# A ViT tower in fp32 on one core: the patch embedding on 64 rows in paired row halves, its bias added apart

## The reference, cut to what matters

```python
h  = patches @ W.T + b                            # (16, 784, 64): the embedding
xn = layernorm(h)                                 # over the 64 features
s_t = tanh(xn_t @ W_ih.T + b_ih + b_hh + s_(t-1) @ W_hh.T)   # scan over the 16 images
h  = h + s
x  = layernorm(h)
logits = x @ gate_w + gate_b                      # top 2 of 16, softmax over the two
e_out[e] = relu(x @ w1[e] + b1[e]) @ w2[e] + b2[e]
y  = x + sum over the 2 chosen e of weight * e_out[e]
out = h + layernorm(y) * gamma + beta
```

## Time and profile before

| | |
|---|---|
| median of 3 runs | 536.03 us |
| profiled execution, whole time | 535.65 us |
| its span in the trace | 533.9 us |
| mean granted clock of TensorE | 0.989 |
| PE busy | 507.5 us, 95% |
| DVE busy | 418.0 us, 78% |
| ACT busy | 350.3 us, 66% |
| POOL busy | 173.6 us, 33% |

### The profile page before, as it was taken

The page is one execution under the profiler, slowest core; times in us unless marked ns, Lnnn a source line. Parts: engine busy times, 40 slices in busy tenths (PEclk is TensorE's granted clock), DMA queues, the critical chain, the costliest instruction groups (busy, mean ns, idle before and its releaser), DMA issues.

```text
span 533.9 us, 8845 instructions
## 1 busy us (share of the span) xinstructions
PE 507.5 (95%) x3044; PEld 338.5 (63%) x3044; DVE 418.0 (78%) x841; ACT 350.3 (66%) x606; POOL 173.6 (33%) x126
## 2 busy tenths in 40 slices
PE   4777999999999999999999999999999999999992
PEld 4454667676766766666676666667676766666652
DVE  1545797896969788796969889696988879797665
ACT  3545575857768586766858675776858577666661
POOL 4220111613424252432335162332426244222223
PEclk9997999999999999999999999999999999999998
DMA  6219175855829194573909476482928456483901
GB/s 142 67 40 221 40 170 130 189 124 121 175 70 229 40 208 102 125 182 93 211 25 206 104 171 144 103 192 63 219 59 187 109 129 151 110 189 77 205 19 30
DMA packets 29755, 69.04 MB, mean 129 GB/s; under 512 B 6432, under 2 KB 8464, under 8 KB 29584
## 3 DMA queue, kind: packets, MB, share of 16 engines
q1 hardware_dynamic: 29712, 68.49, 56.2%
HBM read 60.39 MB, written 8.08 MB: 128 GB/s over the span
## 4 chain that ended last, share of the span: by engine, by line
PE 89%; issue 3%; POOL 2%; DMA 2%; DVE 1%; ACT 1%; POOLq 0%; SPq 0%; DVEq 0%; ACTq 0%
PE pZ L845 37%; PE pO L858 34%; PE pA L871 4%; PE pA L760 3%; PE pA L796 2%; PE pA L814 2%; PE pB L760 2%; PE pA L784 2%; PE pB L826 1%; POOL inv_std L348 1%; DMA spread<-gates_dram 1%; PE pB L814 1%; PE pA L772 1%; PE pA L785 1%; DMA gates_dram<-gt 1%
## 5 line engine op out<-in xcount | busy, mean ns | idle before, releaser
L478 ACT ACTIVATE hexp<-pZ,b1c 128x784 f32<-128x784 f32 x256 | 223.1, 911 | 107.2 <-PE pZ L845 107.1
L858 PE MATMUL pO<-hexp,w2s 128*64 128x392 f32 x1024 | 199.8, 506 | 0.6 <-ACT hexp L478 0.3
L845 PE MATMUL pZ<-xt,w1hi 128*128 128x392 f32 x512 | 189.2, 369 | 1.4 <-ACT xt L405 1.0
L637 DVE SCALAR_TENSOR_TENSOR prod<-pO,b2c,spread 128x392 f32<-128x392 f32 x256 | 149.0, 620 | 42.3 <-PE pO L858 38.6
L845 PE MATMUL pZ<-xt,w1lo 128*128 128x392 f32 x512 | 175.4, 343 | 0.0
L348 POOL TENSOR_TENSOR inv_std<-var,nhalf 112x7 f32<-112x7 f32 x48 | 75.8, 1580 | 198.0 <-DVE var L546 198.0
L845 PEld LDWEIGHTS pZ<-xt,w1hi 128*128 128x128 f32 x512 | 97.2, 190 | 48.1 <-issue 28.7
L858 PEld LDWEIGHTS pO<-hexp,w2s 128*64 128x64 f32 x1024 | 70.3, 136 | 75.9 <-issue 63.1
L653 DVE TENSOR_TENSOR acc<-acc,prod 128x784 f32<-128x784 f32 x111 | 111.3, 1003 | 0.1
L845 PEld LDWEIGHTS pZ<-xt,w1lo 128*128 128x128 f32 x512 | 97.4, 190 | 0.0
L546 DVE TENSOR_REDUCE var<-sq 112x7 f32<-112x455 f32 x48 | 29.9, 624 | 49.2 <-ACT sq L409 36.4
(11 more groups left out here) (95 smaller groups left out, 472.7 us busy)
## 6 DMA issues: line engine op xcount, KB each, us to landing
spread<-gates_dram SPq DMA_DIRECT2D x128, 392.0 KB, 9.0
h_dram<-h SPq DMA_DIRECT2D x16, 248.1 KB, 2.4
h2c<-h_dram SPq DMA_DIRECT2D x16, 248.1 KB, 7.2
xcur<-x_in SPq DMA_DIRECT2D x16, 196.0 KB, 7.2
out<-yo SPq DMA_DIRECT2D x15, 196.0 KB, 7.0
w1f<-w SPq DMA_DIRECT2D x2, 512.0 KB, 5.9
w2s<-w SPq DMA_DIRECT2D x1, 512.0 KB, 3.7
gates_dram<-gt SPq DMA_DIRECT2D x16, 28.0 KB, 2.0
```

Of the source, the lines that this page charges most:

```text
L478: nc.scalar.activation(hexp[u % RING][:, :].rearrange("p (b c) -> p b c", b=2), halves(pZ[u % 2]), ACT.Relu, bias=b1c[:, u:u + 1]).then_in ...
L637: nc.vector.scalar_tensor_tensor(out=prod[q % RING][:, b * HALF:(b + 1) * HALF], in0=halves(pO)[:, b, :], scalar=b2c[:, q:q + 1], in1=spre ...
L845: last = nc.tensor.matmul(halves(pZ[e % 2])[:, b, :], w[:, e, :], xt[par][:, b * HALF:(b + 1) * HALF], start=(k == 0), stop=(k == 1))
L858: last = nc.tensor.matmul(halves(pO)[k * D:(k + 1) * D, b, :], w2s[:, e, :], hexp[e % RING][:, b * HALF:(b + 1) * HALF], start=True, stop= ...
```

## The change: what it does, and the diff

The embedding is over the 64 pixel rows alone. `xcur` has 128 rows: the even tiles' tokens lie on the rows 0 to 63, the odd tiles' on the rows 64 to 127 (the host lays them out in that order, and `load_x` issues two DMAs, of 448 and 336 columns). `tokw` stands on both row halves, made by two products in place of one. The bias, turned through `fold` like the weights, is made by one more product as a tile `tokb` of 112 x 81 and copied by DVE. In the loop ACT still copies the result to `h1`, and POOL then adds `tokb` to it in place (`bias_h1`, ahead of `rstd` of the mix stage). In the prologue DVE does the copy and the addition in one instruction for each bank, in place of ACT's copy. `square_h1` moves from slot 11 to 13 (from 12 in body 0), and the embedding's `norm_var` from slot 13 to 14. The two fills of the row of ones go.

```diff
-        tokw = sb("tokw", [K_IN + 1, W])
+        tokw = sb("tokw", [2 * D, W])
+        tokb = sb("tokb", [P, W])
...
-        xcur = [sb(f"xcur{i}", [K_IN + 1, TOK]) for i in range(2)]
+        xcur = [sb(f"xcur{i}", [2 * D, FIRST]) for i in range(2)]
...
-        fills = [(fold[:, 0:D], -1.0 / D), (fold[:, D:D + 1], 1.0 / D), (xcur[0][K_IN:K_IN + 1, :], 1.0),
-                 (xcur[1][K_IN:K_IN + 1, :], 1.0),
+        fills = [(fold[:, 0:D], -1.0 / D), (fold[:, D:D + 1], 1.0 / D),
                  (ident[:, :], 0.0), (sq[:, :, :, D:D + 1], EPS), (nhalf[:, :], -0.5), (state[:, :, :], 0.0),
                  (gates[:, :, :], 0.0)]
-        FOLD_SET, ONES_SET, EPS_SET, STATE_SET = 4, 6, 8, 10
+        FOLD_SET, EPS_SET, STATE_SET = 4, 6, 8
         RANK_SET, IDENT_SET = len(fills) + 3, len(fills) + 4
...
-                sp.dma_start(xcur[s % 2][0:K_IN, :], x_in[:, bass.ds(s * TOK, TOK)]).then_inc(xload[s % 2], 16)
+                for k, (first, n) in enumerate(((0, FIRST), (FIRST, REST))):
+                    sp.dma_start(xcur[s % 2][k * D:(k + 1) * D, 0:n],
+                                 x_in[:, bass.ds(s * TOK + first, n)]).then_inc(xload[s % 2], 16)
...
+            def bias_h1(s, par):
+
+                pool.wait_ge(h1_kept, 2 * s + 2)
+                nc.gpsimd.tensor_tensor(h1[par][:, :, :], h1[par][:, :, :], over_tiles(tokb[:, :], W), ALU.add)\
+                    .then_inc(h1_biased, 1)
...
+                if embed:
+                    bias_h1(t + 3, 1 - par)
...
-                for some, fresh in zip(some_tiles, embedded_in(s)):
+                for some, fresh in zip(some_tiles, wide):
...
-                act.wait_ge(h1_kept, 2 * (s) + 2)
+                if known(s, 3):
+                    act.wait_ge(h1_kept, 2 * s + 2)
+                else:
+                    act.wait_ge(h1_biased, s - 2)
...
-                    if embed and u == at(t, 11, first=12):
+                    if embed and u == 13:
...
-            nc.scalar.activation(tokw[:, :], pB[0:K_IN + 1, 0:W], ACT.Copy).then_inc(weights_made, 1)
-            keep_h1(0, 0)
+            nc.scalar.activation(tokw[:, :], pB[:, 0:W], ACT.Copy).then_inc(weights_made, 1)
             square_h1(0, 0)
-            keep_h1(1, 1)
             square_h1(1, 1)
             w1_high_part(0)
...
-            keep_h1(2, 0)
...
+            def keep_h1(s, par):
+
+                dve.wait_ge(h1_made, s + 1)
+                if not known(s, 2):
+                    STATE.wait(dve, s - 2, "h2")
+                for some, n, fresh in zip(some_tiles, (PAIRS, TILES - PAIRS), embedded_in(s)):
+                    nc.vector.tensor_tensor(h1[par][:, some, :], fresh, tokb[:, :].unsqueeze(1).to_broadcast([P, n, W]),
+                                            ALU.add).then_inc(h1_kept, 1)
...
-                    if embed and u == 13:
+                    if embed and u == 14:
...
+            dve.wait_ge(weights_made, 3)
+            nc.vector.tensor_copy(tokb[:, :], pA[0:P, 0:W]).then_inc(tokb_made, 1)
+            dve.wait_ge(tokb_made, 1)
+            keep_h1(0, 0)
             dve.wait_ge(consts, EPS_SET)
             norm_var(EMBED, 0, 0)
+            keep_h1(1, 1)
...
+            keep_h1(2, 0)
...
-            nc.tensor.matmul(pB[0:K_IN + 1, 0:W], tokt[:, :], fold[0:D, :], start=True, stop=True)\
-                .then_inc(weights_made, 1)
-            pe.wait_ge(consts, ONES_SET)
+            nc.tensor.matmul(pA[0:P, 0:W], tokt[:, K_IN:K_IN + 1].to_broadcast([D, P]), fold[0:D, :],
+                             start=True, stop=True)
+            for k in range(2):
+                last = nc.tensor.matmul(pB[k * D:(k + 1) * D, 0:W], tokt[:, 0:K_IN], fold[0:D, :],
+                                        start=True, stop=True)
+            last.then_inc(weights_made, 1)
             pe.wait_ge(weights_made, 4)
...
-                pe.wait_ge(xload[s % 2], 16 * (s // 2) + 16)
+                pe.wait_ge(xload[s % 2], 32 * (s // 2) + 32)
...
-                    last = nc.tensor.matmul(embedded_in(s)[i % 2][:, i // 2, :], xcur[s % 2][:, i * P:(i + 1) * P],
-                                            tokw[:, :], start=True, stop=True)
+                    rows = slice((i % 2) * D, (i % 2 + 1) * D)
+                    last = nc.tensor.matmul(embedded_in(s)[i % 2][:, i // 2, :],
+                                            xcur[s % 2][rows, (i // 2) * P:(i // 2 + 1) * P], tokw[rows, :],
+                                            start=True, stop=True)
...
-    x = x.reshape(patch * patch, steps, p, tiles).transpose(0, 1, 3, 2).reshape(patch * patch, -1)
+    x = x.reshape(patch * patch, steps, p, tiles).transpose(0, 1, 3, 2)
+    x = np.concatenate([x[:, :, 0::2], x[:, :, 1::2]], 2).reshape(patch * patch, -1)
```

More of the change, by code:

```diff
@@ L50, in vit_tower_kernel @@
     PARTS = 4
-    assert 2 * D == 128 and PAIRS * W <= 512 and F == 128 and FIRST <= 512 and HALF <= 512 and EVEN * D <= 512
+    assert 2 * D == 128 and K_IN == D and PAIRS * W <= 512 and F == 128 and FIRST <= 512 and HALF <= 512 and EVEN * D <= 512
     assert Q % RING == 0 and (STEPS - 4) % 2 == 0
@@ L161, in vit_tower_kernel @@
         w1_low = sem("w1_low_parts")
+        h1_biased = sem("h1_biased")
+        tokb_made = sem("embed_bias_made")
         weights_made = sem("centred_weights_made")
@@ L746, in _ @@
             pe.wait_ge(weights_made, 2)
-            nc.tensor.matmul(pB[0:K_IN + 1, 0:W], tokt[:, :], fold[0:D, :], start=True, stop=True)\
-                .then_inc(weights_made, 1)
-            pe.wait_ge(consts, ONES_SET)
+            nc.tensor.matmul(pA[0:P, 0:W], tokt[:, K_IN:K_IN + 1].to_broadcast([D, P]), fold[0:D, :],
[4 more added lines that the diff above has]
+            last.then_inc(weights_made, 1)
             pe.wait_ge(weights_made, 4)
+            pe.wait_ge(tokb_made, 1)
             def embed_in(s):
-                pe.wait_ge(xload[s % 2], 16 * (s // 2) + 16)
+                pe.wait_ge(xload[s % 2], 32 * (s // 2) + 32)
                 if known(s, 3) and not known(s, 2):
```

## The result

The changed kernel takes 528.7 us (median of four, 527.15 to 531.6) against 535.57 for the kernel before beside it (534.93 to 537.37): a ratio of 0.9877, interval 0.9853 to 0.99. The profiled execution took 527.49, with a span of 525.4 against 533.9; that is 8.2 us less in time and 8.5 in span. In a second series the unchanged new kernel took 530.26 (five, 527.81 to 530.58) against 535.61, and the median of all nine is 529.9. Both of these lie inside the forecast's range. The miss of 0.5 us is thus within the new kernel's own spread of 4.4, and on which side of the edge a median falls is luck.

What follows compares the result with a forecast made beforehand. PE was taken to bound the kernel: the profiled 535.65 us, less 5.6 for the loop's embeddings, plus 1.1 for the prologue, gave 531.15; the runs' median being 0.38 higher, the forecast was 531.5 us, range 529.5 to 533.

Steps and rivals of the forecast that it cites:

- The embedding in the loop: `embed_in` on PE, 13 times: 1.37 us falls to 0.94 as in `hidden_turn`, 0.43 less per step, 5.6 in all.
- Rival 3: Loop embedding: the pairs overlap without the 0.16 us at the group's ends, total 529.4 us; chance 0.05.
- The bias on POOL and the moves: In the loop: POOL's addition takes 1.8 us (1.2 to 2.6) in idle time; moving square and reduce costs and gains nothing.
- the rule by which the prediction had the two engines take turns: Loop: a DVE instruction with two SBUF inputs and a POOL instruction reading SBUF hold a shared port pair one at a time.
- Rival 4: Loop: the embedding's `rstd` becomes late and holds DVE and PE; 544.5 us at 1.5 us of delay; chance 0.05.
- rival 1: Loop: DVE is the real bound, the gain returns as waits; 537 us if all is lost, 534 if half; chance 0.16.
- The prologue: Before the loop: +1.1 us (0.1 to 1.6), with `scale_h1(0)` and what follows 1.0 later behind the cast of `rank`.
- Rival 2: Prologue costs nothing because the transfers of `gate_loads` land as before; 530.4 to 530.5 us; chance 0.08.
- busy throughout at a granted clock of 1.00: Loop, 30 us from 210 to 240: PE has no idle time at 2.4 GHz, so time taken from it counts in full.

Runs made afterwards that it cites:

- experiments 2 and 3: New kernel, loop embedding unpaired (even tiles issued first, then odd): 533.76 us; new kernel, all embedding tiles on rows 0 to 63: 538.28 us.
- Experiment 6: Filler: eight unread products in PE's wait ahead of step 1's x2 turn; added to the kernel before 533.01 us, to the new kernel 529.48 us.
- its repeat: The new kernel measured again without any edit: 530.26 us, ratio 0.9892 to the kernel before.
- no bias: New kernel without POOL's bias addition in the loop, `square_h1` waiting for the copies alone: 531.22 us.
- old slots: New kernel with `square_h1` back in slot 11 (12 in the first body) and the embedding's `norm_var` back in slot 13: 530.28 us.
- cast later + filler: New kernel with gate-load wait and cast of `rank` behind `scale_h1(1)`, plus eight unread products ahead of step 1's x2 turn: 528.89 us.
- kept warm: New kernel with the later cast and the eight unread products, plus 46 more unread products in PE's prologue waits: 526.96 us.
- cast later: New kernel with the wait for the gate loads and the cast of `rank` moved behind `scale_h1(1)` on DVE: 529.62 us.
- experiment 7: Kernel before with each image's pixels x loaded by two DMAs: 535.93 us; the same with eight unread products ahead of step 1's x2 turn: 533.59 us.

## Why the prediction was right and where it was not

- **The embedding in the loop** (0.43 us a step, 5.6 in all): right in mechanism and size. It measures 0.43 in the weight loads and 0.44 in the step; experiments 2 and 3 show that pairing is its only source. The trace gives 4.55 + 0.87 = 5.42, less than 13 x 0.44 by one step of 30.48 us, below. Rival 3 (no price at the ends) falls with the 0.257 us behind the last load.
- **The bias on POOL and the moves** (nothing): right. The addition is shorter than forecast in the mean, 1.46 us, and leaving it out changes no step. Where it began 0.2 us or more ahead of the end of DVE's addition to `acc`, five times of 13, POOL waited as the prediction said: it took 1.38 to 1.86 us and ended 1.16 to 1.18 behind the end of `acc` (237.13 and 238.30 in one case, where it began at 236.49), and `acc` kept its 0.97 us. The other eight took 1.30 or 1.31. But the rule by which the prediction had the two engines take turns does not hold for every pair: in the kernel before, `acc` ran from 98.02 to 98.99, its usual 0.97 us, beside POOL's `rstd` from 97.12 to 98.60. Rival 4 did not come; the embedding's `rstd` has 1.48 us, as others.
- **DVE** (rival 1): not the bound. Its wait for PE ahead of the product is 1.5 us in the new kernel's window from 210 to 240, 1.96 before, 0.4 less as forecast, and it has not been used up.
- **The prologue** (+1.1): +1.05 at `scale_h1(0)` and at the gates' store, through the cast behind `gbias`, which starts 1.33 us later. The part ahead of it is right too: the first embedding starts 0.94 us later (5.84 and 6.78), and its copy still comes no later (8.78 and 8.67). Rival 2, that the transfers would land as before, is out.
- **What failed is the sum**: the step "Sum of the prologue: +1.1" was added as if it were all that could change before the loop settles, and PE's clock was read in the loop alone ("busy throughout at a granted clock of 1.00"). In the first 50 us the clock was not at 1.00 throughout. From the x2 turn of step 1 the kernel before takes 2.96 us longer in its traced execution than the new one does. Experiment 6 confirms it at 2.6 us by taking away the idle time ahead of it. The traced execution of the new kernel does not pay it; three others with the same prologue pay 1.6 us. So the clock of the start stood at nothing in the sum, without a reason, and was worth up to 3 us. A further 1.24 came from the way of the gates through DRAM.

The Trainium skill (TensorE: Matmul & The Clock Gate, What's actually happening) describes TensorE as throttled by default and released by activity; the traces agree, with 0.53 us a product until 34 or 42 us and 0.34 behind it. In the traces without the filler, the ones in which PE had idled for 2.1 to 2.8 us ahead of the x2 turn have the low stretch behind it, and the two in which it had idled for 0.91 and 1.32 do not. So a wait of PE near the start can cost its own length once more, here 2.96 us behind 2.77. That rival, with a price of up to 3 us, was missing.

**What stays open.** Why the clock rises between 34 and 37 us in some executions and near 42 in others, also with the same prologue; and what makes up the part of the spread that does not go with the mean clock. Why the way of the gates takes 2.46 us in some traces (the new kernel, its repeat, no bias, old slots, cast later + filler, kept warm) and 3.2 to 3.84 in others (before, before + filler, new + filler, unpaired, rows 0-63, cast later, before with x in two DMAs), and in a form of the kernel before (x in two DMAs + filler) 2.48: it follows no part of the change, so I don't count its 1.24 us as the change's. And therefore how much of the 6.9 us is the change's own: 4.2 to 5.0 with the filler in both at like clocks, 5.4 in the repeat. Of the forecast's two terms the loop's 5.6 is shown; the prologue's 1.1 is shown at the gates' store, and in the time it is known only as the 0.6 to 1.3 of experiment 7.

## What to carry to other kernels

A short matmul group on half the rows gains by pairing tiles on the two row halves, not by its fewer rows: count the places of issue, add a fixed price at the end of the group (0.16 us here), and compare. One row beyond 64 (here the ones for a bias) can be worth moving to an idle engine for that. Before summing an edit of 1%, read the clock row slice by slice, and the lengths of equal products beside it, since here it read 1.00 over products of 0.53 us. Where they are not level, executions of one kernel can differ by as much as the edit brings, here from 525.1 to 529.5 us of span, so one trace of each side does not price the start. Unread products in PE's wait are a cheap way to hold the clock there in both kernels while the rest is compared.

## What was not expected of the hardware

In the tenth full step of every variant of the new kernel, and in none of the kernel before, DVE starts a product 0.20 us late without waiting for anything that the trace shows:

```profile
375.80 0.27 DVE L625 SCALAR_TENSOR_TENSOR lg<-best,lg 112x112 f32<-112x112 f32 x1
376.27 1.16 DVE L658 SCALAR_TENSOR_TENSOR prod<-pO,b2c,spread 128x392 f32<-128x392 f32 x2 [0.20 <-issue]
```

In that stretch, the one without slack of the earlier trace rows, PE pays for it at once: the step is about 0.27 us longer than its neighbours, 30.48 in place of 30.21 in the new kernel. SP's issue of the two x loads lies beside it and lasts 2.02 us in place of about 1.2, but it is not the cause. In the kernel kept warm it lasts 1.15 us at that place, and the 0.20 is there all the same; in the kernel before with x in two DMAs it lasts 2.21, and DVE is not late:

```profile
382.49 2.21 SPq L249 DMA_DIRECT2D xcur<-x_in  x2
...
383.66 1.15 DVE L639 SCALAR_TENSOR_TENSOR prod<-pO,b2c,spread 128x392 f32<-128x392 f32 x2
```

What the cause is stays open.
